# The recurrent stage of a two-layer block as a wavefront: halves of the sequence over the layers

## The reference, cut to what matters

```python
xn = _layernorm(x)
h = einsum('blv,dv->bld', xn, Win) + bin              # 512 -> 64 channels
for l in range(4):                                     # lax.scan over the layers
    y = silu(layernorm(h, ln1_w, ln1_b))
    y = sconv(y, phazor, last_conv)                    # causal convolution along the sequence
    h = h + y * sc_lin
    y = layernorm(h, ln2_w, ln2_b)
    y = silu(einsum('bld,fd->blf', y, W1) + b1)        # 64 -> 256
    h = h + einsum('blf,df->bld', y, W2) + b2          # 256 -> 64
s = einsum('bld,vd->blv', layernorm(h, lnl_w, lnl_b), Wout) + bout
g = silu(xn @ W.T + bias + low-rank updates)           # 512 -> 512
x = x + s * g
```

## Time and profile before

| | us |
|---|---|
| median of 3 runs (727.61 to 730.28) | 728.43 |
| the profiled execution's own time | 725.75 |
| its span | 723.82 |
| block A and the barrier, to | 467.2 |
| head of block B, to the first `center` of the loop | 502.7 |
| four layers, to | 695.4 |
| last norm, to | 704.1 |
| outputs and last DMA, to the end | 723.8 |

### The profile page before, as it was taken

The page is one execution under the profiler, slowest core; times in us unless marked ns, Lnnn a source line. Parts: engine busy times, 40 slices in busy tenths (PEclk is TensorE's granted clock), DMA queues, the critical chain, the costliest instruction groups (busy, mean ns, idle before and its releaser), DMA issues. The chain is left out here.

```text
span 723.8 us, 9105 instructions
## 1 busy us (share of the span) xinstructions
PE 638.7 (88%) x2756; PEld 459.0 (63%) x2756; DVE 518.8 (72%) x959; ACT 332.7 (46%) x559; POOL 236.1 (33%) x339
## 2 busy tenths in 40 slices
PE   5798999999999999999999989847789587786976
PEld 4677878888888888888888865724334233332432
DVE  6898897877887878877878766795744826628528
ACT  5678384384374474573572662103144152251340
POOL 1000010010010010010020099670465776685767
PEclk9899999999999999999999999977989699698788
DMA  8711002002002002002001080000000000000006
GB/s 295 264 40 59 1 0 88 1 0 87 0 0 87 0 0 87 0 0 87 0 1 58 8 293 30 23 22 11 2 0 11 0 0 11 0 11 0 0 1 232
DMA packets 17594, 32.78 MB, mean 45 GB/s; under 512 B 3392, under 2 KB 3904, under 8 KB 17568
## 3 DMA queue, kind: packets, MB, share of 16 engines
q1 hardware_dynamic: 17568, 32.47, 12.8%
HBM read 25.13 MB, written 7.34 MB: 45 GB/s over the span
## 5 line engine op out<-in xcount | busy, mean ns | idle before, releaser
L743 DVE TENSOR_SCALAR_CACHE_REDUCE junk_d<-k_buf,cand 128x1376 int8<-128x1376 f32 x56 | 91.8, 1640 | 0.3
L574 ACT ACTIVATE junk_a<-k_buf,cand 128x1376 int8<-128x1376 f32 x56 | 80.5, 1437 | 0.6
L1007 PE MATMUL ps_a<-wd_hi,zt_hi 128*128 128x512 f32 (+1 forms) x176 | 71.8, 408 | 1.9 <-DVE zt_lo L856 1.0
L488 POOL TENSOR_TENSOR rstd<-var_eps,expo 128x2 f32<-128x2 f32 x8 | 5.6, 705 | 203.6 <-DVE var_eps L684 203.6
L496 POOL TENSOR_TENSOR xres<-xres,gate 128x512 f32<-128x512 f32 x12 | 23.6, 1964 | 144.5 <-DVE gate L863 144.5
L555 ACT ACTIVATE s_buf<-ps_a 128x1376 f32<-128x1376 f32 x16 | 21.1, 1319 | 106.0 <-PE ps_a L980 103.6
L1007 PE MATMUL ps_a<-wd_hi,zt_lo 128*128 128x512 f32 (+1 forms) x176 | 69.1, 393 | 0.0
L1007 PE MATMUL ps_a<-wd_lo,zt_hi 128*128 128x512 f32 (+1 forms) x176 | 69.0, 392 | 0.0
L1614 PE MATMUL ps_t<-arena 128*128 128x512 f32 x128 | 67.6, 659 | 0.0
L980 PE MATMUL ps_a<-wg_hi,xt_hi 128*128 128x512 f32 (+1 forms) x192 | 53.0, 385 | 1.2 <-DVE xt_lo L672 1.2
L980 PE MATMUL ps_b<-wu_hi,xt_hi 128*128 128x512 f32 (+1 forms) x192 | 52.4, 381 | 0.0
(11 more groups left out here) (194 smaller groups left out, 1412.0 us busy)
## 6 DMA issues: line engine op xcount, KB each, us to landing
xin<-in_x SPq DMA_DIRECT2D x8, 512.0 KB, 3.6
xres<-in_x SPq DMA_DIRECT2D x8, 512.0 KB, 3.5
out<-arena SPq DMA_DIRECT2D x16, 256.0 KB, 2.1
x_scratch<-xres SPq DMA_DIRECT2D x6, 512.0 KB, 3.0
arena<-x_scratch SPq DMA_DIRECT2D x3, 1024.0 KB, 11.7
m_buf<-in_wd_t SPq DMA_DIRECT2D x3, 512.0 KB, 9.2
m_buf<-in_wg_t SPq DMA_DIRECT2D x2, 688.0 KB, 5.3
k_buf<-in_wg_t SPq DMA_DIRECT2D x2, 688.0 KB, 7.8
```

Source lines behind the costliest of these rows:

```text
L488: pool.tensor_tensor(rstd[:], var_eps[:], expo[:], ALU.pow).then_inc(ln_rs, 1)
L574: act.activation(junk_a[:], k_buf[:, 1, :], ACT.Sign, bias=c, scale=-1.0, accum_out=below[:, 1:2]).then_inc(act_step, 1)
L743: dve.tensor_scalar(junk_d[:], k_buf[:, 0, :], c, -float(DROP), ALU.is_lt, ALU.add, accum_out=e).then_inc(cnt_dve, 1)
L1007: last = pe.matmul(ps_a[:, t, :], zs, ws[0:rows, c, :], start=(c == 0 and n == 0), stop=(c == CHUNKS - 1 and n == 2))
```

## The change

- The four iterations of the loop become ten **phases**, written out. Phase p has a mixing part (first norm, convolution) of layer p // 2 and half p % 2, and a feeding part (second norm, up, down) of the layer and half that were mixed in phase p - 1. Phase 0 has only mixing, phases 8 and 9 have the last norm and 8 outputs each in place of mixing, and phase 9 has no feeding. All semaphores of this part are doubled, one for each half.
- On every engine the mixing part's step comes first, then the feeding part's.
- The **tables** have 512 positions in place of 1024 (32 fine and 16 coarse powers). Half 1 uses the same tables, since the scan's state is multiplied by a power of p at the boundary: four operations of 128x1 on VectorE (`hand_over`), whose result is the start of the scans of half 1. The six table operations of a layer stand half behind the convolution of one phase and half behind that of the next.
- The **bias rows**: `f_bias` and `bout` enter the sums in PSUM by a matmul of float32r operands, ones times a row split in a high and a low part. That takes away `gate_bias` (VectorE, 16 operations), `bias_out` (GpSimd, 32) and x1's wait for it, and adds 32 matmuls, and for the split one operation of 128x1024 on each of GpSimd (a memset), ScalarE and VectorE, two of 1x1024 on ScalarE, and 8 small DMAs.
- The gate reads `xt` in place, without `take_tokens` (ScalarE, 16 operations), and has banks of its own (`bankg`); `GATES = (2, 3, 1, 3, 1)` is ten steps, two tiles, in each of phases 1 to 7, and the last two tiles stand after phase 7.
- In the head, the 11-step root becomes one `pow` on GpSimd (`root_tokens`), and the second 8 tiles go into other buffers, so that half 0 of layer 0 begins while they are on their way. All weights of the four layers are loaded at once.

```diff
-GATES = (1, 2, 1, 7, 1, 2, 2)
+PHASES = 2 * DEPTH + 2
+GATES = (2, 3, 1, 3, 1)
...
+            def mixing(phase):
+                return phase // 2, phase % 2
+            def feeding(phase):
+                return (phase - 1) // 2, (phase - 1) % 2
...
+                root_tokens(2)
+                tables(0, 0, 6)
+                root_tokens(3)
+                for phase in range(PHASES):
...
+                    root(2 * l, c)
+                    if 0 < phase < PHASES - 1:
+                        root(2 * k + 1, d)
+                    if l < DEPTH:
...
+                        times_sin(l, c, y, ln_o, 2 * l + 1, cv_wi)
+                        times_sin(l, c, u_im, cv_ui, l + 1, cv_b)
+                        if l + 1 < DEPTH:
+                            tables(l + 1, 3 * c, 3 * c + 3)
...
+                def hand_over(l):
+                    a, b = u_re[:, NB - 1:NB], u_im[:, NB - 1:NB]
+                    re, im = e_c[:, 0, l:l + 1], e_c[:, 1, l:l + 1]
+                    dve.wait_ge(cv_ui[0], l + 1)
+                    dve.tensor_scalar(part[:, 0:1], a, re, None, ALU.mult).then_inc(cy_t, 1)
...
+                    variance(q, c)
+                    if feeds:
+                        variance(n, d)
+                    widen(q, c)
+                    normed(q, c)
+                    if feeds:
+                        widen(n, d)
+                        normed(n, d)
+                    if l < DEPTH:
+                        turn(l, c)
+                        scan(l, c, False)
+                        scan(l, c, True)
+                        turn_back(l, c)
+                        if c == 0:
+                            hand_over(l)
+                        into_h(l, c)
...
+                    elif feeds:
+                        fed(k, d)
+                    if phase == 0:
+                        h_in(1)
...
+                    if n == 0:
+                        if k >= 2:
+                            pe.wait_ge(g_done, k - 1)
+                        pe.matmul(bankg[k % 2], ones_r[0:DIM, :], row_r[0:DIM, 0, :], start=True, stop=False)
+                        return
...
+                    center_rows(q, c)
...
+                    if feeds:
+                        center_rows(n, d)
+                    gates(GATES[0])
+                    variances(q, c)
+                    if feeds:
+                        variances(n, d)
+                    gates(GATES[1])
+                    spread(q, c)
+                    gates(GATES[2])
+                    if feeds:
+                        spread(n, d)
+                        gates(GATES[3])
...
+                    if phase == PHASES - 3:
+                        gates(TILES * (KH + 1))
+                    for m in outs[2:]:
+                        output(m)
```

More of the change, by code:

```diff
@@ L1340, in _ @@
-                pool.wait_ge(last_in, 16 * 5)
-                layer(0, False, True)
-                with pool.Fori(1, DEPTH - 1) as l:
-                    layer(l, True, True)
-                layer(DEPTH - 1, True, False)
-                for k in range(4):
-                    bias_out(DEPTH - 1, k)
-                for c in range(HALVES):
-                    root(2 * DEPTH, c)
-                for m, t in enumerate(OUT):
+                    pool.tensor_tensor(w_im[:, cs(c)], src[:, cs(c)], rot_s[:, l, :], ALU.mult).then_inc(done[c], 1)
@@ L1410, in _ @@
[L1410 to L1422 removed]
+                    act.wait_ge(ln_y[c], q + 1)
@@ L1513, in into_h @@
+                    dve.wait_ge(cv_ab[c], l + 1)
                     dve.scalar_tensor_tensor(out=h[:, cs(c)], in0=w_re[:, cs(c)], scalar=pcol(l, C_SCL),
[L1514 to L1546 removed]
@@ L1585, in _, with project_in @@
-                pe.wait_ge(mk, N_MK)
+                def project_in(c):
+                    pe.wait_ge(win_in, 16)
+                    pe.wait_ge(xt_a, 12 if c else 4)
+                    pe.wait_ge(xt_v, 4)
+                    for k in range(KH):
+                        for b in range(BATCH):
+                            last = pe.matmul(bank1[c][b * DIM:(b + 1) * DIM, :], win[:, k, :],
+                                             xt[:, k, b * SEQ + c * NB:b * SEQ + (c + 1) * NB],
+                                             start=(k == 0), stop=(k == KH - 1))
+                    last.then_inc(h_ps[c], 1)
@@ L1681, in _, with output @@
-                q = 2 * DEPTH
-                for part in (center_rows, variances, spread):
-                    for c in range(HALVES):
-                        part(q, c)
-                for m, t in enumerate(OUT):
-                    if m % 8 == 0:
-                        pe.wait_ge(ln_o, 2 * q + m // 8 + 1)
-                    if m >= 4:
-                        pe.wait_ge(o_used, m - 3)
+                        last.then_inc(ff_2[c], 1)
+                def output(m):
+                    t = ORDERED[m]
@@ new lines, in output @@
+                    pe.matmul(output_bank(m), ones_r[rows, :], row_r[rows, 1, :], start=True, stop=False)
+                    pe.matmul(output_bank(m), y[rows, j * P:(j + 1) * P], wout[rows, :],
+                              start=False, stop=True).then_inc(o_ps, 1)
+                pe.wait_ge(mk, N_MK)
+                for i in range(8):
+                    tokens(i)
+                project_in(0)
+                tokens(8)
+                tokens(9)
+                steps = iter(range(TILES * (KH + 1)))
```

660 lines of the change are left out of this document (319 added, 341 removed).

## The result

| | before | after |
|---|---|---|
| median, us (3 runs each) | 728.43 | 706.01 (705.31 to 706.41) |
| ratio | | 0.9686, 95% interval 0.9655 to 0.9718 |
| span of the profiled execution | 723.8 | 704.0 |
| last matmul of block A starts at | 464.40 | 466.37 |
| from there to the end | 259.4 | 237.6 |

The account below looks back on a forecast made before the run. Layers were taken as bound by a chain with no engine full, the head by VectorE. High-clock terms reached 695.0 us; 7 for the clock gave a 702.0 span, and a 706.6 median; 701 to 714 at 0.57, range 696 to 724.

Parts of the forecast that it names:

- phase 0: First phase, from h of half 0 at 485.5 us to 507.8, mixing only: 22.3 us.
- phase 1, with the clock: The phase after TensorE's 9.7 us standstill: 20.3 us at the high clock, plus 4.5 for the low clock.
- phases 6 and 7, both: Last two layer phases, without table steps: `into_h` 1.4 us in place of 3.4, so 18.4 each.
- in the layout already: Removing `gate_bias`, `bias_out` and `take_tokens` from VectorE, GpSimd and ScalarE was given no separate gain.
- A middle phase: A phase laid out on all engines: 20.3 us, with 7.65 on TensorE first; gates, not the root, delay the spread.
- The cover: In a middle phase TensorE's line is 17.3 us; down ends 3 us early, so the convolution covers the feeding part.
- The head: Start of block B: first transpose at 470.4 us, projection 3.65, h at 485.5, 10 us sooner than before.
- The clock: Low TensorE clock costs 7 us: 4.5 in phase 1, 1 in the head, 1.5 in the outputs.
- A: Rival: the clock falls in each of phases 2 to 7, 3 us each, 18 in all: 724.6 us; chance 0.18.
- B: Rival: no clock loss, and GpSimd's table steps miss `into_h`: 690 to 700 us; chance 0.12.
- C: Rival: TensorE becomes the bound, each phase growing by 5 us at the low clock: about 740; chance 0.08.
- D: Rival: mixing and feeding parts don't overlap, a phase takes 25 us: about 737; chance 0.05.

Follow-up runs that it names:

- e9: The kernel before with `bias_out` left out, so `bout` is not added: 714.7 us, against 729.1 for the kernel before beside it.
- e5: The changed kernel with only the wavefront undone, both halves side by side through a layer, other parts kept: 705.1 us.
- e2: The changed kernel with one gate matmul moved from ahead of the first spread to behind the second, and ScalarE's Silu behind both `norm_out`s: 701.3 us.
- e3: The changed kernel with the two gate tiles from behind phase 7 moved into TensorE's idle time ahead of phase 1: 695.8 us.
- e4: The changed kernel without the tables of layers 1 to 3; all layers use layer 0's: 699.4 us.
- e7: The changed kernel with the head reordered: constants awaited after ten tiles, statistics and copies earlier on VectorE, `norm_out` ahead of ScalarE's last copies in phase 0: 696.9 us.
- e1: The changed kernel with one gate matmul moved from ahead of the first spread to behind the second, ScalarE's Silu not moved: 705.9 us.
- e6: The changed kernel without the bias rows' matmuls, so neither `f_bias` nor `bout` is added: 700.7 us.
- e8: The changed kernel with e2 and e3 joined and four outputs of phase 8 put into the norm of phase 9: 692.6 us.
- e11: e10 plus six 128x512 matmuls that nobody reads, on TensorE in phase 9: 683.9 us.
- e10: The changed kernel with all edits that gained, mended and joined, one gate tile ahead of phase 1 and one in phase 8: 684.9 us.
- e12: e10 plus three edits in phases 8 and 9: last gate tile and its Silu earlier, an update of h earlier, a GpSimd sum later: 677.1 us.

## Why the prediction was right, point by point

The time was right to 0.6 us, and the span to 2.0 us, of which block A's later end (466.37 for 464.40) is 1.97. That end was no step of mine: at 434.9, in code that both kernels share, four records of 128x512 matmuls took 3.62 us behind an idle time of 2.55, where before they took 1.99. That the time came closer than the span is luck: I added 2.7 us because the profiled execution of before lay that far below its median, and that of after is its median. The steps from the start of block B on sum to 234.8 in the forecast and in the profile, because their errors cancel. One is arithmetic: the terms of a phase as I listed them add up to 20.2, and to 18.2 without table steps, where I wrote 20.3 and 18.4.

| step | forecast | measured | |
|---|---|---|---|
| start of block B to h of half 0, with the clock | 19.3 | 19.5 | right |
| phase 0 | 22.3 | 20.4 | y 1.0 earlier; `into_h` 2.1, not 3.4 |
| phase 1, with the clock | 24.8 | 21.8 | low clock cost 2.0, not 4.5 |
| phases 2 to 5, each | 20.3 | 19.84 | see below |
| phases 6 and 7, both | 36.8 | 41.5 | TensorE is the bound, and the clock |
| gate tiles behind phase 7 | 6.4 | 7.2 | rows at 0.43 |
| phase 8 | 21.7 | 23.8 | both norms 9.3, not 7.6; clock 0.86 |
| phase 9 to the last sum, with the clock | 19.7 | 18.7 | |
| to the end | 2.6 | 2.5 | right |

- **The bound, and what carries it.** That a chain with two waits bounded the layers was read rightly, and e9 shows that I gave the credit to the wrong part: `bias_out` and `gate_bias` went as "in the layout already", and the overlap of mixing and feeding got all of it, though e5 without that overlap is as fast (705.1). The step that failed is the attribution; the sum was of a laid-out phase, so it didn't feel it.
- **A middle phase.** The gates, not the root, are what the spread waits for: right (e2). The head of a phase took 8.3 (550.80 to 559.07), not 7.65: the bias row and its gate matmul took 1.39 and not 1.09, since the row costs 0.43 to the next matmul (552.72 to 553.15) where I had taken 0.23 from two like ones, and the two centers took 1.92 and not 1.72. `into_h` took 2.9, not 3.4, and what lies between (559.07 to 566.95) 7.9, not 8.4.
- **The cover.** "Down ends 3 us before the phase does" was wrong: it ends 0.8 before the update (569.02, 569.81). TensorE's line is 18.2 us to the end of down, not 17.3: 0.6 in the head of the phase, and 0.5 in the gate matmul between the up units and the second two of these, which took 1.06 and 1.42. This mis-sized line is why phases 6 and 7 gained 0.8 from having no table steps, not 1.9 (18.4 forecast, 19.05 at the high clock in e3), and why a phase without table steps gives 0.8 and not 1.5 (e4).
- **The head.** First transpose 2.9 behind the barrier's end for 3.2, memset 0.95 for 1.1. The projection took 5.35 at the low clock, the four normalizations 4.70 for 6.4. That ScalarE's two single-row copies stand ahead of `norm_out` was right: VectorE waits 3.93 us there. What I wrote of the barrier, that no engine works from 464.8 to 467.2, holds for TensorE and ScalarE only: VectorE and GpSimd finish block A's last tile there, until 466.85.
- **The clock.** 7 us forecast. What rows show, against the same phases at the full clock in e3: 2.0 in phase 1, 1.7 each in phases 6 and 7, 0.7 in phase 8, together 6.1 and something in the head. The right size for partly the wrong places. The skill's rule (the Trainium skill, TensorE: Matmul & The Clock Gate, Terms: throttled time times the share withheld) fits phase 1 if one counts the time in which matmuls ran: low from 509.15 to 513.3, 4.1 us, so 2.1 by the rule and 2.0 measured. The clock was low from 503.1 on, though, and by all 10.2 us the rule gives 5.1. My input to it, 25 us, held such idle time.
- **The rivals.** A, the clock falling in every phase at 3 us each: it fell in two of six, for 1.7 each. B no: table steps do hit `into_h`. C no as priced, but its mechanism, TensorE as the bound, holds in phases 6 and 7, even at the full clock. D no: the phases are 20 long, not 25. The rival that I didn't have is that the wavefront, with its ends unfilled, gives nothing over the other parts.

## What to carry to other kernels

Split a change with many parts by undoing its headline, not by adding up its parts: here the headline was worth nothing as it stood, and the quiet part (32 operations of an idle-looking engine), left out alone, two thirds of the gain. A pipeline over halves saves inside and pays at both ends, so give its first and last stage something to do: fillers behind the last stage belong into the idle time ahead of the first. A filler inside a chain has to be over, on every engine that it touches, when the chain's next operand comes. When a filler moves on one engine, look at what its result stands in front of on the next engine.

## What the runs showed of the hardware

- The clock falls in some middle phases and not in others with the same list. In all thirteen falls below, the first slow matmuls are the gate matmuls right behind the variances of 128x2; in phase 3 these ran at full clock (six records in 2.82 us at 555.81, above). The changed kernel in phase 6:

```profile
613.61 0.95 PE L1621 MATMUL ps_a<-means,arena 128*128 128x2 f32 x8
614.42 1.03 PE L1621 MATMUL ps_b<-means,arena 128*128 128x2 f32 x8
615.31 4.52 PE L1642 MATMUL ps_b<-arena,xt 128*128 128x512 f32 x6
```

  Phases that fell, of 2 to 7, in the profiles: 6 and 7 in the changed kernel and in e7, 4, 6 and 7 in e1, 5 in e2, none in e3, e6, e8 and e11, 5 and 6 in e4, 2 in e10, 3 and 4 in e12. Each cost 1.6 to 1.8 us. In e12, phases 2 and 3:

```profile
518.30:537.20 18.90, 17.70 (x62) 7.86 (x62) 10.20 (x14) 7.30 (x12) 9.80 (x8) 1.00 0.00 0
537.20:557.90 20.70, 19.45 (x63) 8.59 (x63) 10.71 (x17) 7.30 (x12) 9.91 (x8) 0.92 0.00 1
```

  That one or two such falls make up much of the spread of a kernel's runs (673.6 to 679.6 in e12) is likely and not shown, since each kernel has one profile. What triggers them stays open.
- A float32r matmul of 64x512 ahead of a float32 one costs 0.43 us to the next start, 0.34 between outputs, against 0.23 between like ones.
- ScalarE's copy of 1x1024 takes 1.07 us, as long as that of 128x1024 (1.05).
